# A decoder kernel: the Relu experts' hidden layer computed transposed with its gates as bfloat16 parts, and the capacity experts' third row tile computed as two column tiles side by side

## The reference

```python
def _L1_ffn_ref(x, expert_sel, keys, values, route_scale):   # 16 experts of 64 hidden units, 4 chosen
    sel_probs = sigmoid(einsum('btd,ed->bte', x, expert_sel))
    _, sel_index = top_k(sel_probs, 4)
    sel_val = take_along_axis(sel_probs, sel_index, axis=-1)
    sel_val = sel_val / clip(sel_val.sum(-1, keepdims=True), 1e-09) * route_scale
    scores_all = relu(einsum('btd,edh->bteh', x, keys))
    values_all = einsum('bteh,ehv->btev', scores_all, values)
    return (take_along_axis(values_all, sel_index[..., None], axis=2) * sel_val[..., None]).sum(axis=2)

def _L3_ffn_ref(inputs, gate_w, w1, w2):                     # 8 experts, hidden 1024, capacity 320 rows
    probs = softmax(tokens @ gate_w); expert_idx = argmax(probs)
    # each token goes to a slot of its expert, tokens past the 320th of an expert are dropped
    h = relu(einsum('ecd,edf->ecf', expert_input, w1))
    expert_output = einsum('ecf,efd->ecd', h, w2)
    out = einsum('tec,ecd->td', combine_weights, expert_output)
```

## Time and profile before

| | us |
|---|---|
| median of 3 runs | 3391.46 (3388.67 to 3393.8) |
| profiled execution, time | 3394.49 |
| profiled execution, span | 3392.7 |
| PE busy | 3077.6 (91%) |
| DVE busy | 1659.0 (49%) |
| ACT busy | 1222.0 (36%) |
| POOL busy | 291.9 (9%) |

### The profile page before, as it was taken

The page is one execution under the profiler, slowest core; times in us unless marked ns, Lnnn a source line. Parts: engine busy times, 40 slices in busy tenths (PEclk is TensorE's granted clock), DMA queues, the critical chain, the costliest instruction groups (busy, mean ns, idle before and its releaser), DMA issues. The chain is left out here.

```text
span 3392.7 us, 56135 instructions
## 1 busy us (share of the span) xinstructions
PE 3077.6 (91%) x22954; PEld 1959.4 (58%) x22954; DVE 1659.0 (49%) x2939; ACT 1222.0 (36%) x2636; POOL 291.9 (9%) x511
## 2 busy tenths in 40 slices
PE   6999899999989998899999988989999899889695
PEld 3665566666658885556666655656655333346463
DVE  4665344444433234534444443225556999957112
ACT  1332244455431112235544441113323666623011
POOL 1111000000000000000000000000011000001102
PEclk9999999999999999799999999989999999989797
DMA  2001000000100002000000000000001000000432
GB/s 104 18 13 62 9 1 1 1 1 1 60 16 0 0 0 85 15 1 1 1 1 1 1 26 28 12 31 23 10 26 38 16 1 1 1 19 14 150 130 86
DMA packets 36410, 85.14 MB, mean 25 GB/s; under 512 B 3246, under 2 KB 30103, under 8 KB 32599
## 3 DMA queue, kind: packets, MB, share of 16 engines
q1 hardware_dynamic: 31831, 75.06, 6.3%
q0 software_dynamic: 1536, 4.20, 0.4%
q10 hardware_dynamic: 2816, 2.62, 0.2%
HBM read 53.90 MB, written 9.44 MB: 19 GB/s over the span
## 5 line engine op out<-in xcount | busy, mean ns | idle before, releaser
L2329 ACT ACTIVATE prob<-R,neg_max 128x333 f32<-128x333 f32 x512 | 268.8, 538 | 182.3 <-DVE neg_max L2399 182.3
L3420 DVE TENSOR_TENSOR_SCAN arena<-arena,u 128x512 f32<-128x512 f32 x256 | 289.5, 1201 | 0.1
L2399 DVE TENSOR_REDUCE neg_max<-R 128x2 f32<-128x666 f32 x256 | 205.6, 845 | 97.0 <-PE R L2209 97.0
L2220 PEld LDWEIGHTS T<-const,prob 128*128 128x128 f32 (+1 forms) x1536 | 183.3, 143 | 96.3 <-issue 66.2
L2405 DVE COPY prob_t<-T 128x384 f32<-128x384 f32 x256 | 141.6, 553 | 188.4 <-PE T L2220 183.2
L2220 PE MATMUL T<-const,prob 128*128 128x128 f32 (+1 forms) x1536 | 210.0, 273 | 19.7 <-DVE prob_t L2405 19.5
L2336 ACT ACTIVATE prob_t<-T 128x384 f32<-128x384 f32 x256 | 126.3, 493 | 213.2 <-PE T L2220 206.6
L3351 ACT ACTIVATE arena<-delta,neg_a 128x510 f32<-128x510 f32 x256 | 177.2, 717 | 46.7 <-DVE arena L3420 45.7
L2169 PE MATMUL O<-arena,keys_in 128*128 128x512 f32 (+1 forms) x384 | 183.8, 603 | 5.0 <-ACT arena L2310 2.4
L2164 PE MATMUL O<-keys_in,arena 128*128 128x333 f32 x512 | 170.3, 458 | 1.2 <-DVE arena L2380 1.2
L3257 PE MATMUL R<-arena,diag 64*64 64x512 f32 x1024 | 136.1, 622 | 24.6 <-DVE arena L3420 24.4
(11 more groups left out here) (463 smaller groups left out, 5488.1 us busy)
## 6 DMA issues: line engine op xcount, KB each, us to landing
w<-w_dram SPq DMA_DIRECT2D x16, 1024.0 KB, 7.1
arena<-pack_dram SPq DMA_DIRECT2D x2, 4100.0 KB, 15.0
q_pad<-q_pad SPq DMA_DIRECT2D x24, 224.0 KB, 2.7
arena<-pack_dram SPq DMA_DIRECT2D x4, 1284.0 KB, 6.0
arena<-pack_dram SPq DMA_DIRECT2D x1, 4896.0 KB, 15.3
arena<-k_nat SPq DMA_DIRECT2D x16, 224.0 KB, 2.7
arena<-arena SPq DMA_DIRECT2D x16, 224.0 KB, 2.8
arena<-pack_dram SPq DMA_DIRECT2D x1, 2707.0 KB, 14.8
```

The lines of the kernel that those rows point to most:

```text
L2220: last = nc.tensor.transpose(S.T[0:n, i, kc * P:(kc + 1) * P], prob[:, g % 2, i, first:first + n], S.ident)
L2329: last = nc.scalar.activation(prob[:, g % 2, i, :], S.R[:, g % 2, i * BANK:i * BANK + XK], ACT.Exp, bias=neg_max[:, g % 2, i:i + 1], accum ...
L2399: nc.vector.tensor_reduce(neg_max[:, g % 2, :], S.R[:, g % 2, :].rearrange("p (i n) -> p i n", i=2)[:, :, 0:XK], AX.X, ALU.max, negate=Tru ...
L3420: nc.vector.tensor_tensor_scan(state[:, q % HELD, :], decay[:, q % DEEP, :], u[:, i % 2, :], 0.0, ALU.mult, ALU.add)\
```

## The change

In the Relu stage the hidden layer is computed with the keys as the stationary operand and `x_t` as the moving one, so it comes out with hidden units in partitions and needs no transposes. The gates must then lie across partitions: they are split into three bfloat16 parts whose sum is the float32 gate, transposed once for all tokens at the head (16 transposes into four banks, four ACT copies), and spread over each expert's 64 hidden units by a matmul with a matrix of zeros and ones (`expand`, new in the weights of the stage, `[48 rows used] x 1024`). ACT copies the spread gates to SBUF, since the product reads the hidden layer from PSUM. The batches are unrolled and pipelined over three: hidden of i, outputs of i-1, layer norm and transposes of i-2. The normalised x is written to `x_nat` directly, and SP's copies into `xc` are gone. The chain of the gates multiplies once after the compare instead of four times.

In the capacity stage the third row tile's matmuls take 128 columns of w2 each and are twice as many. One half is written to partitions 0 to 63, the other to 64 to 127 of the same 128 columns. ACT copies both at once and stores them with two DMAs.

```diff
 def moe_relu(nc, S, k):
+    G = HC // 2            # 4 groups of 2 x 128 hidden units; a bank of R each
+        hid = sb("hid", [P, 2, HC, T])
+        gates = sb("gates", [P, 2, 2, BANK])
+        def hidden_bank(g):
+            return S.R[:, g % 2, g // 2 * BANK:(g // 2 + 1) * BANK]
         # sync
-            sync_x(nc, S, sp, 0)
             prefetch(nc, S, sp, k + 1)
-            with sp.Fori(1, B) as b:
-                sync_x(nc, S, sp, b)
         # tensor
+            def hidden(b, g):
+                if b >= 1:
+                    pe.wait_ge(M.exp_done, G * (b - 1) + g + 1)
+                for h in range(2):
+                    for c in range(C):
+                        last = nc.tensor.matmul(hidden_bank(g)[:, h * T:(h + 1) * T], keys[:, c, (2 * g + h) * P:(2 * g + h + 1) * P],
+                                                S.x_t[:, c, b * T:(b + 1) * T], start=(c == 0), stop=(c == C - 1))
+                last.then_inc(M.s_full, 1)
+            def spread(b, half):
+                if b >= 1 or half:
+                    pe.wait_ge(M.kg_ready, 2 * b + half)
+                for h in range(4):
+                    c = 4 * half + h
+                    last = nc.tensor.matmul(S.T[:, h // 2, h % 2 * T:(h % 2 + 1) * T], expand[:, c * P:(c + 1) * P],
+                                            gate_t[:, b * T:(b + 1) * T], start=True, stop=True)
+                last.then_inc(M.st_full, 1)
+            def outputs(b):
+                pe.wait_ge(M.exp_done, G * (b + 1))
+                if b >= 1:
+                    pe.wait_ge(M.y_read, b)
...
+            def transposed(b):
+                pe.wait_ge(M.yn_ready, b + 1)
...
             pe_logits(nc, S, pe, part(W, TB, "sel", C))
+            hidden(0, 0)
             pe_logits_by_token(nc, S, pe, logits_t)
+            for g in range(1, G):
+                hidden(0, g)
+            keep_warm(nc, S, S.T[:, 1, :], 11)
+            settle(pe, M.setup, 1)
+            for j, bank in enumerate(banks):
+                for i in range(4):
+                    last = nc.tensor.transpose(bank[0:64, i * P:(i + 1) * P], gate_wide[:, 4 * j + i, :], S.ident)
+                last.then_inc(M.k_full, 1)
+            settle(pe, M.k_sb, len(banks))
+            for i in range(B + 2):
+                if i < B:
+                    spread(i, 0)
+                    for g in range(G):
+                        if i >= 1:
+                            hidden(i, g)
+                        if g == 1:
+                            spread(i, 1)
+                if 0 <= i - 1 < B:
+                    if i == B:
+                        keep_warm(nc, S, hidden_bank(0), 2)
+                    outputs(i - 1)
+                if 0 <= i - 2 < B:
+                    if i == B + 1:
+                        keep_warm(nc, S, hidden_bank(0), 7)
+                    transposed(i - 2)
+            keep_warm(nc, S, hidden_bank(0), 2)
         # scalar
+            def spread(b, half):
+                act.wait_ge(M.st_full, 2 * b + half + 1)
+                if b >= 1:
+                    act.wait_ge(M.exp_done, G * (b - 1) + 2 * half + 2)
+                nc.scalar.activation(gates[:, half, :, :], S.T[:], ACT.Copy).then_inc(M.kg_ready, 1)
...
+            for i in range(B + 2):
+                if i < B:
+                    spread(i, 0)
+                    spread(i, 1)
+                if 0 <= i - 2 < B:
+                    transposed(i - 2)
         # vector
+            def clipped(b, g):
+                dve.wait_ge(M.s_full, G * b + g + 1)
+                dve.wait_ge(M.kg_ready, 2 * b + g // 2 + 1)
+                nc.vector.scalar_tensor_tensor(hid[:, b % 2, 2 * g:2 * g + 2, :].rearrange("p c t -> p (c t)"), hidden_bank(g), 0.0,
+                                               gates[:, g // 2, g % 2, :], ALU.max, ALU.mult).then_inc(M.exp_done, 1)
...
+            for i in range(B + 2):
+                if i < B:
+                    clipped(i, 0)
+                    clipped(i, 1)
+                if 0 <= i - 2 < B:
+                    normalised(i - 2)
+                if i < B:
+                    clipped(i, 2)
+                    clipped(i, 3)
+                if 0 <= i - 1 < B:
+                    result(i - 1)
 def moe_capacity(nc, S, k, out):
         # tensor
-                for t, n in ROWS:
+                for t in range(2):
                     for f in range(FC):
-                        last = nc.tensor.matmul(S.O[0:n, t // 2, (t % 2) * D:(t % 2 + 1) * D], hid[:, f, t * P:t * P + n], w2[:, s, f, :],
+                        last = nc.tensor.matmul(S.O[:, 0, t * D:(t + 1) * D], hid[:, f, t * P:(t + 1) * P], w2[:, s, f, :],
                                                 start=(f == 0), stop=(f == FC - 1))
-                    if t == 1:
-                        last.then_inc(S.y_full, 1)
+                last.then_inc(S.y_full, 1)
+                for f in range(FC):
+                    for h in range(2):
+                        last = nc.tensor.matmul(S.O[h * HB:(h + 1) * HB, 1, 0:P], hid[:, f, 2 * P:CAP], w2[:, s, f, h * P:(h + 1) * P],
+                                                start=(f == 0), stop=(f == FC - 1), skip_group_check=True)
                 last.then_inc(S.v_full_act, 1)
         # scalar (ye_stored now counts 48 for three DMAs, before 32)
-                nc.scalar.activation(ye[0:n, s, 2, :], S.O[0:n, 1, 0:D], ACT.Copy).then_inc(S.o_free[1], 1)
+                nc.scalar.activation(ye[:, s, 2, 0:P], S.O[:, 1, 0:P], ACT.Copy).then_inc(S.o_free[1], 1)
                 act.drain()
-                act.dma_start(S.ye_dram[bass.ds(e * CAP + 2 * P, n), :], ye[0:n, s, 2, :]).then_inc(S.ye_stored[s], 16)
+                for h in range(2):
+                    act.dma_start(S.ye_dram[bass.ds(e * CAP + 2 * P, HB), h * P:(h + 1) * P], ye[h * HB:(h + 1) * HB, s, 2, 0:P])\
+                        .then_inc(S.ye_stored[s], 16)
```

More of the change, by code:

```diff
@@ L2829, in _ @@
             keys, values = part(W, TB, "keys", C), part(W, TB, "values", HC)
[L2830 to L2843, removed]
@@ L2888, in _ @@
+            keep_warm(nc, S, hidden_bank(0), 2)
+            settle(pe, M.kg_ready, 2 * B)
+            settle(pe, M.exp_done, G * B)
+            settle(pe, M.y_read, B)
+            settle(pe, M.yn_ready, B)
+            settle(pe, M.xt_done, B)
         @block.scalar
@@ new lines, in result @@
+            def result(b):
+                dve.wait_ge(M.y_full, b + 1)
+                nc.vector.tensor_tensor(ysb[:, b % 2, :, :], S.O[:, 0, :].rearrange("p (t d) -> p t d", t=TT),
+                                        S.x_nat[:, b * TT:(b + 1) * TT, :], ALU.add).then_inc(M.y_read, 1)
+                dve.drain()
+                for tt in range(TT):
+                    nc.vector.bn_stats(bst[:, tt, :], ysb[:, b % 2, tt, :])
+                dve.drain()
+                for tt in range(TT):
+                    last = nc.vector.bn_aggr(mv[:, b % 2, tt, :], bst[:, tt, :])
+                last.then_inc(M.ln_stat, 1)
@@ L2909, in _, with normalised @@
+            def normalised(b):
+                dve.wait_ge(M.rstd_ready, b + 1)
+                for tt in range(TT):
+                    last = nc.vector.tensor_scalar(S.x_nat[:, b * TT + tt, :], ysb[:, b % 2, tt, :], mv[:, b % 2, tt, 0:1],
+                                                   rstd[:, b % 2, tt:tt + 1], ALU.subtract, ALU.mult)
+                last.then_inc(M.yn_ready, 1)
             dve.wait_ge(S.weights_ready[k], 16)
-            each = [P, NT, E]
+            nc.vector.memset(gate_wide[:, :, 3 * E:64], 0.0)
@@ L2950, in _ @@
+            settle(dve, M.s_full, G * B)
+            settle(dve, M.y_full, B)
+            settle(dve, M.rstd_ready, B)
         @block.gpsimd
         def _(pool):
-            with pool.Fori(0, B) as b:
-                tail_pool(nc, S, pool, b)
+            for b in range(B):
+                pool.wait_ge(M.ln_stat, b + 1)
+                nc.gpsimd.tensor_scalar(rstd[:, b % 2, :], mv[:, b % 2, :, 1], EPS, None, ALU.add)
+                pool.drain()
+                nc.gpsimd.tensor_tensor(rstd[:, b % 2, :], rstd[:, b % 2, :], part(S.const, CONST, "neg_half")[:, 0:TT], ALU.pow)\
+                    .then_inc(M.rstd_ready, 1)
```

147 lines of the change are left out of this document (69 added, 78 removed).

## The result

The changed kernel takes 3356.51 us (median of four runs, 3350.86 to 3361.01) against 3392.04 for the kernel before (3388.67 to 3393.8 in four): a ratio of 0.9896 with a 95% interval of 0.9877 to 0.9914. The forecast was 3357.7. The profiled execution took 3361.01 us, with a span of 3359.1.

The account below looks back on a forecast made before the run. PE, busy for 91% of the span, was taken to bound the kernel. Savings of 20.7 us (Relu stage) and 13.1 (capacity) took the profiled 3394.5 to 3360.7, less 3.0 to the median: 3357.7, range 3350 to 3370.

Parts of the forecast that it names:

- The batch: Steady Relu batch on PE: hidden 6.98, outputs 6.98, transposes 0.44, two spread blocks of 0.60; 15.6 us, formerly 18.44.
- The head: Start of the Relu stage: gates ready at 2072.4 us, PE running without a gap from 2079.3.
- The fall of the clock: First new Relu batch: one fall of PE's clock as before, adding 3.2 us, bounds 0 and 6.4.
- The end: Relu stage's end: last outputs done at 2200.4, PE reaches the last transposes at 2206.4, next stage starts at 2209.1.
- The overhang: Before the Relu stage's last transposes: 14 keep-warm instructions take 6.0 us, so PE reaches the transposes 1.6 us late.
- the 4.9 us: Seven old Relu batches took 4.9 us beyond 7 x 18.44, as falls of PE's clock; predicted gone without gaps.
- The column tiles: Capacity stage, third row tile: 32 instructions side by side take 1.9 us, formerly 3.60; 13.1 saved, bounds 1.76 and 3.6.
- the signs: What would show it right: in the capacity loop, an expert's period falls by 1.7 us and the 32 instructions span 1.9.
- A: Capacity stage: the column tiles don't overlap, 3.6 us for the third tile, only the Relu stage gains; 3371 us, chance 0.07.
- B: New Relu loop: one wait is late, a gap of 1.4 us in each of 7 batches; 3368 us, chance 0.07.
- C: Steady Relu batches: short blocks keep PE at 1.2 GHz, 109 us more; 3467 us, chance 0.02.
- D: Relu stage: gains nothing because its end is set by something else; 3391 us, chance 0.02.

Follow-up runs that it names:

- same_batch: Changed kernel with outputs of a batch straight after its own hidden groups, layer norm and transposes one batch behind: Relu stage 161.99 us, kernel 3363.69.
- trimmed: Changed kernel with two keep-warm fillers at the Relu stage's head, a shorter wait for ACT's copies and fewer keep-warm matmuls at its end: stage 149.00 us, kernel 3353.63.
- head_warm: Changed kernel with one keep-warm matmul in each of two PE waits at the Relu stage's head: stage 152.46 us, kernel 3358.76.
- relu_only: Changed kernel with the capacity stage of the kernel before: Relu stage 155.16 us, kernel 3369.98, ratio to before 0.9945.
- old_loop_filled: Kernel before with one keep-warm matmul between the hidden tile's transposes and the outputs in each Relu batch: Relu stage 168.29 us, kernel 3382.82.
- tiles_in_turn: Changed kernel with the third row tile's 32 matmuls reordered, all of one column tile before the other: capacity stage 247.74 us, kernel 3367.94.
- changed_third: The changed kernel run again, unaltered, beside a repeat of the trimmed version: Relu stage 155.22 us, kernel 3356.89.
- changed_again: The changed kernel run again, unaltered, for comparison in the same rounds: Relu stage 155.04 us, kernel 3354.94.

## Why the prediction was right

**The batch.** Predicted 15.6 us, measured 15.72. The spread blocks themselves cost 0.53 and 0.54. The excess of 0.07 that the prediction put on each of them for the change of shape stands in the group ahead, and is 0.09: hidden 3.65 against 3.56, transposes 0.53 against 0.44. So it is 0.18 a batch for 0.14, and each half of the hidden layer takes 0.07 more than half of the 6.98 that the prediction had for it. Each of the new waits in the loop was hidden, as argued from the time to spare (2.5 us for the tightest, over 2 predicted); same_batch shows what one late product costs.

**The head.** From the stage's first matmul, the gates were predicted ready after 19.2 us (2072.4 less 2053.17) and were after 18.8; the steady loop was predicted after 26.1 and began after 25.2 (2081.75). The fall of the clock was put at 3.2; batch 1 took 18.16 us (2081.75 to 2099.91), and in trimmed, at full clock, 15.29 (2085.40 to 2100.69), so 2.9, and head_warm got 2.7 us back. The rows that the 3.2 stood for gave 3.05 (10.19 less 7.14).

**The end.** From the last outputs' end to the last transposes 6.4 us were predicted (0.44 and 6.0) and are 6.44. The overhang was undersized: the prediction took the old 4.82 as what the layer norm needs and so got 1.6, but x_nat is ready 3.99 after the outputs' end, and PE comes 2.45 behind it. It doesn't touch the sum, since the keep-warm matmuls set this length either way. The whole stage: -20.7 predicted, -21.3 in the two traces, -21.5 in relu_only.

**The reason for the 4.9 us.** The prediction took the falls of the clock inside the old batches to go "since there is no gap". That held, and old_loop_filled shows it as cause: the gap filled, with nothing else changed, the falls are gone. It also shows what the prediction didn't say: with the head's 3.0, some 8 of the change's 21 us were to be had in the old form with one dummy matmul a batch. The rest, 13 us (168.29 to 155.3), is what the transposed form itself brings.

**The column tiles.** Predicted 1.9 us, measured 1.90; eight times the difference to 3.60 is 13.6, less 0.5 for the tail, which came as 4.85 against 4.36. Predicted -13.1, measured -13.5 over all executions. The period of an expert fell by 1.67 (21.28 to 19.61), as the signs asked. The two rows of side-by-side tiles that the price was taken from the earlier trace rows carried over to a shape that neither had.

**The rivals.** A: refuted by the 1.90 us, and tiles_in_turn shows that it is the order that lets the tiles overlap. B: no wait in the steady batches (the idle time of 1.12 us that ends at 2081.75 is the head's); made on purpose it costs 7 us. C: the clock was 1.00 in every stretch behind the head. D: the stage's end moved with its work.

**The total.** The profiled execution was predicted at 3360.7 us and took 3361.0. That is closer than the parts: the touched stages gave 35.5 us where 33.8 were predicted, and the untouched ones took 1.9 back by their scatter. The 0.3 us between forecast and measurement are luck; the parts, each within 1.5 us, are not. The next stage began at 2211.84 and not near 2209, since this one began 3.35 us later than before.

## What to carry to other kernels

A transposed form that saves transposes lives on the price of what it must add: here the same spreading costs 0.53 us a block in bfloat16 parts and 1.92 in float32, and that alone decides whether the stage gains 21 us or loses 4. Before a loop with a short gap on PE is rebuilt, put one matmul that nobody reads into the gap: it tells what of the loss is the clock's (here 8 us of a stage in which the rebuilt loop saved 21). When tiles are placed side by side in the array, alternate them instruction by instruction, and judge edits of a few us by the length of their own stage, not by the total.

## What the runs showed of the hardware that was not expected

- The order of instructions over two column tiles changes their price from 0.059 to 0.102 us each. Even in turn, 32 of them with 128 columns moving (3.26 us) are a little cheaper than 16 with 256 (3.60).
- Gaps of 1.37 and 0.63 us per batch of 18.4 went with falls of the clock in three of seven batches that cost 5.3 us together; with the larger gap cut to 0.46 there were none, nor with one of 0.78 in a batch of 16.8.
- Float32 matmuls with 64 rows and 256 columns take 0.24 us an instruction (1.92 for eight, with the change of shape to the next group in it), not less than the 0.218 of 128 rows: fewer rows save nothing here.
- Untouched stages move by some 17 us between executions of the same kernel (changed_third reaches the Relu stage at 2044.4, changed_again at 2061.8), while the Relu stage repeats within 0.3.
